# Eight stages of a four-layer block turned into two interleaved sequences of steps, with PSUM banks assigned by function

## The chip, the core and the metric

The kernel runs on one core of one Trainium2 chip. The metric is the device time of one execution in microseconds (us). The core's engines each work through their own instruction list in order and meet only at semaphores: TensorE (PE; its weight loads are shown as PEld), VectorE (DVE), ScalarE (ACT), GpSimd (POOL) and SyncE (SP), which here only issues DMAs. Matrix products land in PSUM, which has eight banks of 128 x 512 f32.

## The reference

The batch has 16 sequences of 128 tokens, 128 wide, with a context of the same shape. Four layers follow one another; each is a cross-attention and an FFN, each with a layer norm in front and a residual behind.

```
x = x + xattn0(ln(x), ctx)   # 8 heads of 64, softmax, output product
x = x + ffn0(ln(x))          # 8 experts of 64, top 2 by softmax, plus a shared one, silu
x = x + xattn1(ln(x), ctx)   # 16 heads of 8, softmax, no output product
x = x + ffn1(ln(x))          # 128-512-128, silu; inputs and weights quantized fp4 in blocks of 16
x = x + xattn2(ln(x), ctx)   # 16 heads of 8, masked softmax, output product
x = x + ffn2(ln(x))          # 128-128; fp8, ONE scale from the maximum over the whole tensor
x = x + xattn3(ln(x), ctx)   # 8 heads of 16, weights 1 + tanh(score), output product
x = x + ffn3(ln(x))          # rms norm, int8 rows, ternary weights, gelu, 128-512-128
```

Only the fp8 scale of ffn2 needs all sequences at once. Everything else is done sequence by sequence, so a sequence may be in layer 2 while another is in layer 0.

## The kernel before

The work is cut into one item for each sequence, 16 in all. There are **eight stages**, in the order of the reference, and a stage takes all 16 items before the next one starts, except that the first two items of a stage (EARLY) are mixed into the tail of the one before. Inside a stage `pipeline` (L212) unrolls the first four items, runs the middle in a hardware loop (Fori) of four steps a turn with addresses and semaphore values in registers, and unrolls the tail. In an attention stage the step k handles the projections of item k, the row maxima of item k-2, the probabilities of item k-3 and the output of item k-4.

Attention 1 and 2 compute every score twice. Once queries by keys (L414), from which DVE takes the row maxima (L1310, four of 128 x 512 for one item); and once keys by queries (L430), where the negative maximum is added by a second product with a selection matrix (L435), so that the exponential (L808, ACT) can be read straight from PSUM. The value products are L463. The f32 queries and keys are split into three bf16 parts (L854, L1325, L1021, L1023), written to DRAM by SP, and read back in stacked form. The keys and values of the context for all of layers 1 to 3 are projected in stage 0 (L587, L600) and prepared by DVE (L1399, L1420). Layer norms: DVE takes the statistics (L1279, L1281, L1283), POOL the inverse root (L994), DVE writes the normalized tile (L1288).

In ffn1 the block scales are computed on DVE (`block_scales`, L1143), the blocks are rounded in turn by POOL (L1059, L1049 to L1053) and DVE (`binades`, L1167, L1169 to L1173). In ffn2 DVE normalizes, takes maxima, POOL reduces them over the partitions (L1087), DVE quantizes (L1175).

PSUM: banks 0 and 1 take scores, 2 and 3 alternate for the transposed scores, 4 (and 5) values, 5 to 7 the rest; each stage deals them anew.

## Time and profile before

| what | value |
|---|---|
| median of 3 runs | 979.79 us (979.66 to 981.98) |
| profiled execution, first to last instruction (span) | 977.3 us |
| DVE busy | 629.9 us, 64% |
| PE busy | 614.2 us, 63% |
| ACT busy | 342.3 us, 35% |
| POOL busy | 329.3 us, 34% |
| DMA, mean share of 16 engines | 19.3% on the data queue |

The span is 2.5 us under the median of the runs. No engine is the bottleneck of the whole: the shares are averages over stages that are bound by different engines, so the profile is best read stage by stage. Roughly, from where each stage's own lines are busy, attention 0 runs to about 205 us, ffn0 to 318, attention 1 to 424, ffn1 to 592, attention 2 to 735, ffn2 to 779, attention 3 to 862, and ffn3 to 972.

### The profile page before, as it was taken

To read this page: it belongs to the slowest core of one execution; us is meant where nothing else is said; L and a number is where in the kernel's file an instruction comes from. 1 tells how busy PE (TensorE), PEld (TensorE's weight loads), DVE (VectorE), ACT (ScalarE), POOL (GpSimd) and SP (SyncE) were. 2 spreads that over 40 slices of the span, in tenths; PEclk is the share of its full clock that TensorE was granted. 3 is DMA by queue.
4 is the path that set the end of the run, shared out by engine and by line. 5 is a ranking of instruction groups with operands and counts; after the bars stand their busy time and mean duration, and the time that the engine had idled before them with its cause. 6 is when DMAs were issued, how large, how long until landed. Compare 5 with 4: busy or idle time off the path is not lost.

```text
span 977.3 us, 19947 instructions
## 1 busy us (share of the span) xinstructions
PE 614.2 (63%) x5798; PEld 435.2 (45%) x5804; DVE 629.9 (64%) x2044; ACT 342.3 (35%) x797; POOL 329.3 (34%) x560
## 2 busy tenths in 40 slices
PE   5699999878886899922122227999981276722331
PEld 3588888754444666601010015777750154511110
DVE  2576767637773788778888865666646523267774
ACT  2255555522221465521111112444430134422332
POOL 2112111145553222146656553222100123255441
PEclk9799999979996899965555556999995569955555
DMA  8422232200001344200000012322300135300001
GB/s 247 93 64 58 60 71 56 50 8 1 0 0 33 90 98 97 66 9 0 0 0 0 0 26 64 82 70 64 73 15 0 33 107 136 105 1 0 0 0 43
DMA packets 99780, 46.96 MB, mean 48 GB/s; under 512 B 82992, under 2 KB 92272, under 8 KB 99696
## 3 DMA queue, kind: packets, MB, share of 16 engines
q1 hardware_dynamic: 99728, 46.34, 19.3%
q8 instruction: 24, 0.39, 0.2%
q14 instruction: 28, 0.23, 0.1%
HBM read 26.39 MB, written 19.92 MB: 47 GB/s over the span
## 4 chain that ended last, share of the span: by engine, by line
PE 36%; issue 22%; DVE 13%; POOLq 11%; POOL 10%; DVEq 4%; ACT 2%; DMA 1%; SPq 0%; ACTq 0%
PE bank L463 3%; POOL stats L994 3%; PE bank L430 2%; PE bank L492 2%; PE bank L435 2%; PE bank L446 2%; PE bank L414 2%; POOLq L1050 2%; POOLq L1052 2%; POOL small L1072 2%; PE bank L424 2%; POOLq L1055 2%; POOL att_t L1059 2%; PE bank L565 2%; PE bank L487 1%
## 5 line engine op out<-in xcount | busy, mean ns | idle before, releaser
L994 POOL TENSOR_TENSOR stats<-stats,half_neg 128x1 f32<-128x1 f32 x112 | 63.3, 565 | 251.1 <-DVE stats L1283 243.8
L808 ACT ACTIVATE probs<-bank 128x512 f32<-128x512 f32 x160 | 95.2, 597 | 88.3 <-PE bank L435 87.6
L1310 DVE TENSOR_REDUCE mx<-bank 128x4 f32<-128x512 f32 x160 | 108.1, 680 | 9.7 <-PE bank L414 9.1
L430 PE MATMUL bank<-q_stack,k_stack 128*128 128x128 bf16 x512 | 72.6, 222 | 1.5 <-DVE shift_t L1344 1.4
L435 PE MATMUL bank<-shift_t,sel_bf 128*128 128x128 bf16 x512 | 72.2, 221 | 0.0
L657 PE MATMUL bank<-ident_bf,probs 128*128 128x128 bf16 x16 | 4.6, 286 | 105.5 <-POOL probs L1053 105.5
L1021 POOL CAST q_parts<-resid 128x128 bf16<-128x128 f32 x48 | 14.4, 300 | 149.5 <-DVE resid L1325 149.5
L1288 DVE TENSOR_SCALAR xn<-x_sb,stats 128x128 f32 (+1 forms) x96 | 37.3, 389 | 35.4 <-POOL stats L994 35.1
L1325 DVE SCALAR_TENSOR_TENSOR resid<-bank,w_bias_cols,q_parts 128x128 f32<-128x128 f32 x48 | 16.8, 350 | 64.6 <-ACT q_parts L854 63.9
L1294 DVE TENSOR_TENSOR x_sb<-bank,x_sb 128x128 f32 (+1 forms) x64 | 18.5, 289 | 61.9 <-PE bank L570 26.6
L430 PEld LDWEIGHTS bank<-q_stack,k_stack 128*128 128x128 bf16 x512 | 50.1, 99 | 7.4 <-issue 5.8
L463 PE MATMUL bank<-probs,v_slot 128*9 128x128 f32 x1024 | 52.4, 275 | 1.3 <-ACT probs L808 1.3
L414 PE MATMUL bank<-k_stack,q_stack 128*128 128x128 bf16 x512 | 50.4, 230 | 1.1 <-DMA q_stack<-scratch_q 0.8
L657 PEld LDWEIGHTS bank<-ident_bf,probs 128*128 128x128 bf16 x16 | 1.7, 104 | 110.9 <-POOL probs L1053 105.6
L435 PEld LDWEIGHTS bank<-shift_t,sel_bf 128*128 128x128 bf16 x512 | 50.8, 99 | 0.0
L487 PE MATMUL bank<-w_ident,xn 128*128 128x128 f32 x64 | 21.9, 342 | 45.2 <-DVE xn L1288 45.2
L751 PE MATMUL bank<-ident_bf,yq 128*128 128x128 bf16 x16 | 4.6, 286 | 69.7 <-DVE yq L1650 69.7
L904 ACT ACTIVATE yq_t<-bank 128x128 bf16<-128x128 bf16 x16 | 4.4, 277 | 120.8 <-PE bank L657 120.8
L414 PEld LDWEIGHTS bank<-k_stack,q_stack 128*128 128x128 bf16 x512 | 39.4, 104 | 14.6 <-issue 5.9
L840 ACT ACTIVATE xn_t<-bank 128x128 f32<-128x128 f32 x64 | 17.7, 277 | 80.2 <-PE bank L487 80.2
L1279 DVE BATCH_NORM_STATS2 stats<-x_sb 128x6 f32 (+1 forms) x112 | 32.6, 291 | 13.4 <-DMA x_sb<-in_x 5.8
L859 ACT ACTIVATE att<-bank 128x512 f32<-128x512 f32 (+1 forms) x48 | 25.2, 526 | 39.2 <-PE bank L463 39.2
(272 smaller groups left out, 1845.5 us busy)
## 6 DMA issues: line engine op xcount, KB each, us to landing
k_stack<-scratch_k SPq DMA_DIRECT2D x48, 192.0 KB, 3.4
q_stack<-scratch_q SPq DMA_DIRECT2D x48, 192.0 KB, 3.2
scratch_k<-k_parts SPq DMA_DIRECT2D x48, 96.0 KB, 1.8
scratch_q<-q_parts SPq DMA_DIRECT2D x48, 96.0 KB, 1.8
scratch_k<-k_parts SPq DMA_DIRECT2D x48, 64.0 KB, 1.6
scratch_q<-q_parts SPq DMA_DIRECT2D x48, 64.0 KB, 1.8
scratch_k<-k_parts SPq DMA_DIRECT2D x48, 32.0 KB, 1.5
scratch_q<-q_parts SPq DMA_DIRECT2D x48, 32.0 KB, 1.6
```

Of the source, the lines that this page charges most:

```text
L414: last = mm(dst[:, j * T:(j + 1) * T], q_stack[:, s, h, :], k_stack[:, s, h, :], start=layer == 1, stop=True, skip_group_check=True)
L424: mm(dst[:, j * T:(j + 1) * T], mask_bf[:, s, :], neg_ident[:, :], start=(j == 0), stop=False, skip_group_check=True)
L430: last = mm(o, k_stack[:, s, h, :], q_stack[:, s, h, :], start=layer == 1, stop=False, skip_group_check=True)
L435: last = mm(o, sel[:, h * T:(h + 1) * T], shift_t[:, s, :], start=False, stop=True, skip_group_check=True)
L463: last = mm(bank[4][32 * j:32 * j + w, cols], v, probs[:, (s * U + u) % 4, j * T:(j + 1) * T], start=layer < 3, stop=True, skip_group_chec ...
L487: tr(dst[:, 0:T], xn[:, sA, :], ident[:, :]).then_inc(ln["xnT_ps"], 1)
L808: activation(probs[:, (sP * U + u) % 4, :], bank[2 + u % 2][:, :], ACT.Tanh if layer == 3 else ACT.Exp, scale=float(d) ** -0.5).then_inc(s ...
L859: activation(att[:, sD, 0:U * T], bank[4][:, 0:U * T], ACT.Copy).then_inc(sm["ot"], 1)
L994: tt(stats[:, s, 9:10], stats[:, s, 8:9], half_neg[:, :], ALU.pow).then_inc(ln_rstd, 1)
L1279: nc.vector.bn_stats(stats[:, s, 0:6], x_sb[:, t, :])
L1288: return ts(dst, x_sb[:, t, :], stats[:, s, 6:7], stats[:, s, 9:10], ALU.subtract, ALU.mult)
L1310: reduce(mx[:, sM, u * UNIT:(u + 1) * UNIT], bank[u % 2][:, :].rearrange("p (h k) -> p h k", h=UNIT), AX.X, ALU.max).then_inc(sm["mx"], 1)
```

## The change

The stages and hardware loops are gone; all is unrolled, in **two sequences of steps** with ffn2 between them.

- **First sequence** (28 steps on PE, 29 on ACT, 35 on DVE). In each PE step one item is in attention 0, another in ffn0 three steps behind, another in attention 1 (5 and 6 behind), another in ffn1 (7 to 10 behind) and another in attention 2 (10 to 12 behind). Item b thus meets all five kinds of work within 13 steps. The order of the pieces within a step is written out, and is a different one for each engine.
- **ffn2** afterwards, all 16 items in four groups. Statistics and normalization of a group are done in the first sequence as soon as its items are through.
- **Second sequence** (26 steps on PE): attention 3 and, 7 to 10 steps behind, ffn3.
- **PSUM by function**: banks 0 and 1 scores, 2 transposed scores of every layer, 3 everything that comes in (context and query products, transposes of normalized tiles), 4 everything that goes out, 5 and 6 gate and up products, 7 the rest of the FFNs. `take` makes PE wait for the reader of a bank's last content before it writes there again.
- The shifts by the row maxima are no longer added by a product of their own: two more rows are put into the stacked queries by a DMA and ones into the stacked keys, so that one product with 50 rows gives the shifted score (L526 of the new kernel; L435 goes). The scores for the maxima are done in pairs in the two halves of the rows.
- Keys and values of layers 1 to 3 are projected in each layer's own step (`keys_values`) in place of stage 0, split together with the queries by ACT (`near_parts`, `far_parts`), DVE (`rest`) and POOL (`split`). The biases of values and outputs are added to x by POOL.
- The normalized tiles of the first sequence and of attention 3 are written by ACT (`normalized`) in place of DVE. The sums of attention 0 come from the exponentials' accumulators. The softmax of the router uses ACT's Exp in place of POOL's power.
- The fp4 rounding (`fp4_blocks`) is six DVE operations, POOL has no part in it.

```diff
-        def pipeline(eng, step, last, first=0, early=None, after=0):
...
-            for t in range(first, SLOTS):
-                step(t, t, 0)
-            with eng.Fori(0, B // SLOTS - 1) as i:
-                for j in range(SLOTS):
-                    step(i * SLOTS + (SLOTS + j), SLOTS + j, i + 1)
-            for t in range(B, B + last):
-                step(t, t, t // SLOTS)
-                if early and 0 <= t - B - after < EARLY:
-                    early(t - B - after, t - B - after, 0)
...
-                        last = mm(o, sel[:, h * T:(h + 1) * T], shift_t[:, s, :], start=False, stop=True,
-                                  skip_group_check=True)
...
-            pipeline(pe, attention_step(0), 4, early=ffn0_step(), after=2)
-            turn_weights()
-            pipeline(pe, ffn0_step(), 4, first=EARLY, early=attention_step(1))
-            pipeline(pe, attention_step(1), 4, first=EARLY, early=ffn1_step(), after=2)
-            pipeline(pe, ffn1_step(), 4, first=EARLY, early=attention_step(2))
-            pipeline(pe, attention_step(2), 4, first=EARLY)
-            ffn2(attention_step(3))
-            pipeline(pe, attention_step(3), 4, first=EARLY, early=ffn3_step(), after=2)
-            pipeline(pe, ffn3_step(), 4, first=EARLY)
...
-                        if k == 6:
-                            weights4_round(c - 1)
...
         bank = [ctx.enter_context(nc.psum_tensor(f"bank{i}", [P, 512], F32)) for i in range(8)]
         bank_bf = [b[:, :].bitcast(BF16) for b in bank]
+        SC, ST_BANK, IN_BANK, OUT_BANK = (bank[0], bank[1]), bank[2], bank[3], bank[4]
...
+            def take(name, reader, value):
+                if name in emptied:
+                    pe.wait_ge(*emptied[name])
+                emptied[name] = (reader, value)
...
+                take("in", A[l]["kv"], 2 * item(l, b) + 2)
+                mm(IN_BANK[:, 2 * T:3 * T], proj[:, 2 + l, :], ctx_all[:, b, :], start=True, stop=True)
+                mm(IN_BANK[:, 3 * T:4 * T], ctx_all[:, b, :], proj[:, 5 + l, :], start=True, stop=True
+                   ).then_inc(A[l]["kv_ps"], 1)
...
+                take("st", A[l]["p"], unit(l, b) + u + 1)
...
+                rows = slice(64 * (u % 2), 64 * (u % 2) + 50)
+                for j in range(UNIT):
+                    h = UNIT * (u // 2) + j
+                    done = mm(ST_BANK[:, j * T:(j + 1) * T], stack[l][rows, c, 1, h, :], stack[l][rows, c, 0, h, :],
+                              start=l == 1, stop=True, skip_group_check=True)
+                done.then_inc(A[l]["st"], 1)
...
+            for s in range(28):
+                scores(2, s - 12, 1)
+                values_out0(s - 2, 0)
+                turn(1, s - 5)
+                values_out0(s - 2, 1)
+                query(1, s - 5)
+                hidden_turn_f0(s - 4)
+                scores_t(1, s - 6, 0)
+                down_f1(s - 10)
+                shift_turn(2, s - 12)
+                keys0(s)
+                scores_t(1, s - 6, 1)
+                scores0(s - 1)
+                att_turn0(s - 2)
+                scores_t(1, s - 6, 2)
+                shared_turn_f0(s - 4)
+                values0(s)
+                project0(s - 2)
+                scores_t(1, s - 6, 3)
+                down_f0(s - 4)
+                if s == 6:
+                    for g in range(3):
+                        weights_turn(g)
+                scores_t(2, s - 12, 0)
+                values_out(1, s - 6, 0)
+                values_out(1, s - 6, 1)
+                turn0(s)
+                values_out(1, s - 6, 2)
+                values_out(1, s - 6, 3)
+                scores_t(2, s - 12, 1)
+                turn_f0(s - 3)
+                up_f1(s - 8)
+                scores_t(2, s - 12, 2)
+                route_f0(s - 3)
+                keys_values(2, s - 10)
+                out_turn(1, s - 6)
+                scores_t(2, s - 12, 3)
+                gate_f0(s - 3)
+                turn_f1(s - 7)
+                values_out(2, s - 12, 0)
+                values_out(2, s - 12, 1)
+                scores(1, s - 5, 0)
+                values_out(2, s - 12, 2)
+                values_out(2, s - 12, 3)
+                gate_f1(s - 7)
+                probs_turn0(s - 1, 0)
+                scores(1, s - 5, 1)
+                out_turn(2, s - 12)
+                query0(s)
+                scores(2, s - 11, 0)
+                hidden_turn_f1(s - 9)
+                att_turn2(s - 12)
+                up_f0(s - 3)
+                turn(2, s - 10)
+                shift_turn(1, s - 5)
+                project2(s - 12)
+                query(2, s - 10)
+                probs_turn0(s - 1, 1)
+                if s == 3:
+                    value_bias_product()
+                keys_values(1, s - 4)
+            for s in range(26):
+                turn_f3(s - 7)
+                values_out(3, s - 5, 0)
+                down_f3(s - 10)
+                values_out(3, s - 5, 1)
+                gate_f3(s - 7)
+                hidden_turn_f3(s - 9)
+                project3(s - 5)
+                turn(3, s - 1)
+                query(3, s - 1)
+                scores_t(3, s - 4, 0)
+                keys_values(3, s)
+                scores_t(3, s - 4, 1)
...
+                for j in range(UNIT):
+                    h = u * UNIT + j
+                    done = activation(probs_q[:, u, j * T:(j + 1) * T], SC[u][:, j * T:(j + 1) * T], ACT.Exp,
+                                      scale=float(D0) ** -0.5, bias=mx0[:, b % 2, H0 + h:H0 + h + 1],
+                                      accum_out=sums0[:, b % 2, 2 * j + u:2 * j + u + 1])
+                done.then_inc(A0["ex"], 1)
...
+                act.wait_ge(A[l]["rstd"], j + 1)
+                wait(act, A[l]["xT_ps"], j - 1)
+                activation(xn[l][:, j % 2, :], x_sb[:, b, :], ACT.Identity, bias=stats_a[l][:, j % 4, 10:11],
+                           scale=stats_a[l][:, j % 4, 9:10]).then_inc(A[l]["xn"], 1)
...
+                activation(parts[l][:, j % 2, 0, :, :], qk[l][:, j % 2, :, :], ACT.Copy).then_inc(A[l]["near"], 1)
...
+                activation(parts[l][:, j % 2, 1, :, :], resid[l][:, j % 2, :, :], ACT.Copy).then_inc(A[l]["far"], 1)
...
+            for s in range(29):
...
+                chances_f0(s - 4)
+                turned_f1(s - 8)
+                out_copied(2, s - 13)
+                gate_f0(s - 4)
+                gate_f1(s - 8)
+                normalized(2, s - 11)
+                probabilities0(s - 2, 0)
...
+                normalized_f0(s - 3)
+                probabilities(1, s - 6, 0)
+                far_parts(1, s - 5)
+                probabilities(1, s - 6, 1)
+                hidden_turned_f0(s - 4)
...
+                tt(cols[:, 8:9], cols[:, 7:8], ln_eps[:, :], ALU.add)
+                pool.drain()
+                tt(cols[:, 9:10], cols[:, 8:9], half_neg[:, :], ALU.pow)
+                pool.drain()
+                ts(cols[:, 10:11], cols[:, 6:7], cols[:, 9:10], -1.0, ALU.mult, ALU.mult).then_inc(done, 1)
...
+            def fp4_blocks(src, dst, work, magic, n, sc, rs):
+                tt(blocks(work, n), blocks(src, n), per_block(rs, n), ALU.mult)
+                drain()
+                ts(magic.bitcast(U16), work.bitcast(U16)[:, 1::2], EXPONENT >> 16, None, ALU.bitwise_and)
+                drain()
+                ts(magic, magic, 1.0, FP4_MAGIC, ALU.max, ALU.mult)
+                drain()
+                stt(work, work, -FP4_MAX, magic, ALU.max, ALU.add)
+                drain()
+                tt(work, work, magic, ALU.subtract)
+                drain()
+                return stt(blocks(dst, n), blocks(work, n), FP4_MAX, per_block(sc, n), ALU.min, ALU.mult)
...
+                tt(resid[l][:, j % 2, :, :], qk[l][:, j % 2, :, :], parts[l][:, j % 2, 0, :, :], ALU.subtract
+                   ).then_inc(A[l]["rest"], 1)
```

**ACT.** In the stages of before ACT runs one kind of function at a time. Attention 1 in its loop, one item (`probs` are the probabilities by Exp; `xn_t`, `q_parts` and `att` are copies):

```order
L859 ACTIVATE att<-bank4 128x512
L210 REGISTER_ALU
L804 REGISTER_ALU
L808 ACTIVATE probs<-bank2 128x512
L837 REGISTER_ALU
L840 ACTIVATE xn_t<-bank6 128x128
L210 REGISTER_ALU
L804 REGISTER_ALU
L808 ACTIVATE probs<-bank3 128x512
```

The changed kernel, in a step in which all five kinds of work are under way (`gate` and `gate4` are Silu of ffn0 and ffn1, `probs1` is Exp of attention 1; `oc2` belongs to attention 2, `small` to the router, by Exp):

```order
L1009 ACTIVATE small<-small 128x8
L1048 ACTIVATE yq_t<-bank7 128x128
L980 ACTIVATE oc2<-bank4 128x512
L1017 ACT_TABLE_LOAD
L1017 ACTIVATE gate<-from_x 128x64
L1019 ACTIVATE gate<-bank5 128x512
L1055 ACTIVATE gate4<-bank6,w_scale 128x512
L911 ACTIVATE xn2<-x_sb,stats2 128x128
```

and, 14 rows later in the same step,

```order
L953 ACTIVATE parts1<-qk1 128x256
L994 ACTIVATE xn_f<-x_sb,stats_f 128x128
L968 ACT_TABLE_LOAD
L968 ACTIVATE probs1<-bank2 128x512
L960 ACTIVATE parts1<-resid1 128x256
```

Silu now stands between exponentials, with a table load on each side: 42 table loads in the kernel's list where there were 6. Register instructions and branches are gone.

**DVE.** In before, one step of ffn1, between the scales of two blocks:

```order
L1165 TENSOR_TENSOR small<-small,gs4 128x40
L270 REGISTER_ALU
L1296 ISA
L1296 SCALAR_TENSOR_TENSOR x_sb<-bank7,w_scale,x_sb 128x128
L270 REGISTER_ALU
L1279 ISA
L1279 BN_STATS stats<-x_sb 128x6
L1281 BN_AGGR stats<-stats 128x2
L1283 TENSOR_SCALAR stats<-stats 128x1
L1169 TENSOR_SCALAR att_t<-att_t 128x640
L1171 TENSOR_SCALAR att_t<-att_t 128x640
L1173 TENSOR_SCALAR att_t<-att_t 128x640
```

In the changed kernel, the same place in a full step:

```order
L1379 TENSOR_TENSOR small4<-small4,gs4 128x40
L1655 TENSOR_TENSOR x_sb<-bank7,x_sb 128x128
L1385 TENSOR_TENSOR a4<-src4,small4 128x640
L1387 TENSOR_SCALAR b4<-a4 128x640
L1389 TENSOR_SCALAR b4<-b4 128x640
L1391 SCALAR_TENSOR_TENSOR a4<-a4,b4 128x640
L1393 TENSOR_TENSOR a4<-a4,b4 128x640
L1395 SCALAR_TENSOR_TENSOR dst4<-a4,small4 128x640
L1681 SCALAR_TENSOR_TENSOR src4<-bank5,w_scale,gate4 128x512
```

Six operations of 640 columns stand where three stood; the residual of ffn0 (L1655) lies between two pieces of ffn1.

**PE.** In before, attention 1: transposed scores and shifts in turn, into banks 2 and 3 alternately:

```order
L435 MATMUL bank2<-shift_t,sel_bf 128x128
L537 MATMUL bank5<-w_ident,att 128x128 x4
L476 REGISTER_ALU
L487 MATMUL bank6<-w_ident,xn 128x128
L210 REGISTER_ALU
L414 MATMUL bank0<-k_stack,q_stack 128x128 x4
L430 MATMUL bank3<-q_stack,k_stack 128x128
```

In the changed kernel, near the beginning of a full step (L421 are attention 0's value products, L462 and L470 attention 1's turn and query, L632 and L687 those of ffn0 and ffn1, L360 attention 0's keys):

```order
L462 MATMUL bank3<-w_ident,xn1 128x128
L421 MATMUL bank4<-early,probs0 128x64 x4
L470 MATMUL bank3<-xn_t1,w_proj 128x128
L632 MATMUL bank5<-w_ident,hid 128x128 x4
L526 MATMUL bank2<-stack1 128x128 x4
L687 MATMUL bank7<-wd1_q,hq_t 128x128 x4
L501 MATMUL bank0<-ident_bf,shift2 32x128
L360 MATMUL bank3<-ctx_all,w_wk0 128x128 x4
L526 MATMUL bank2<-stack1 128x128 x4
```

Pieces of five kinds of work follow one another. Consecutive transposed scores (L526) all go to bank 2; between two fills of it stand products of other items.

## Rows read from the trace of the kernel before

**Rows 1.** The windows view by stage: start and end, stretch, busy of each engine.

```profile
core 0: us, PE busy (x) PEld busy (x) DVE busy (x) ACT busy (x) POOL busy (x), PEclk, DMA share, GB/s
0.00:52.00 52.00, 30.99 (x166) 24.20 (x167) 21.11 (x70) 14.92 (x42) 10.93 (x26) 0.87 0.62 165
52.00:205.00 153.00, 142.08 (x1122) 121.57 (x1120) 104.80 (x322) 82.55 (x232) 32.43 (x41) 0.97 0.25 57
205.00:318.00 113.00, 87.52 (x391) 51.41 (x389) 69.95 (x344) 27.55 (x72) 53.62 (x55) 0.89 0.03 8
318.00:424.00 106.00, 90.53 (x1396) 66.07 (x1394) 83.98 (x257) 57.71 (x109) 23.34 (x61) 0.95 0.35 83
424.00:592.00 168.00, 39.01 (x183) 16.85 (x188) 132.19 (x319) 27.19 (x53) 103.47 (x94) 0.50 0.03 7
592.00:735.00 143.00, 133.42 (x1800) 98.32 (x1798) 83.83 (x252) 61.01 (x125) 27.35 (x72) 0.95 0.24 59
735.00:779.00 44.00, 6.80 (x39) 4.41 (x38) 27.84 (x77) 3.68 (x8) 6.33 (x12) 0.50 0.05 13
779.00:862.00 83.00, 53.97 (x555) 38.20 (x556) 26.08 (x107) 32.75 (x77) 25.57 (x69) 0.85 0.40 105
862.00:972.00 110.00, 29.87 (x157) 14.14 (x158) 79.74 (x299) 34.94 (x80) 46.27 (x132) 0.50 0.00 0
```

**Rows 2.** The page, part 4: the chain that ended last, by engine.

```profile
PE 36%; issue 22%; DVE 13%; POOLq 11%; POOL 10%; DVEq 4%; ACT 2%; DMA 1%; SPq 0%; ACTq 0%
```

**Rows 3.** The view by lines: operation, count, busy us and mean ns, idle before.

```profile
L1288 DVE TENSOR_SCALAR xn<-x_sb,stats 128x128 f32 (+1 forms) x96 | 37.3, 389 | 35.4 <-POOL stats L994 35.1
L1288 DVE TENSOR_SCALAR v<-x_sb,stats 128x128 f32 (+1 forms) x16 | 15.8, 987 | 0.7 <-POOL stats L994 0.7
L1283 DVE TENSOR_SCALAR stats<-stats 128x1 f32<-128x1 f32 x112 | 17.2, 154 | 9.2 <-issue 0.8
L1399 DVE TENSOR_TENSOR v<-bank,w_bias_rows 128x128 f32 (+1 forms) x48 | 11.0, 284 | 11.3 <-PE bank L587 11.1
L1385 DVE COPY gated<-bank 128x512 f32<-128x512 f32 x16 | 10.8, 678 | 0.7 <-PE bank L580 0.7
L1420 DVE SCALAR_TENSOR_TENSOR resid<-bank,w_bias_cols,k_parts 128x128 f32<-128x128 f32 x48 | 13.9, 346 | 19.1 <-ACT k_parts L888 19.0
...
L1171 DVE TENSOR_SCALAR att_t<-att_t 128x640 uint32<-128x640 uint32 (+2 forms) x18 | 8.2, 457 | 1.4
L1185 DVE TENSOR_TENSOR tmp_a<-tmp_a,tmp_b 128x512 f32<-128x512 f32 x4 | 2.8, 692 | 0.3
```

**Rows 4.** The view by lines, shapes apart, one line in two shapes.

```profile
L1153 DVE TENSOR_SCALAR small<-small 128x40 uint32<-128x40 uint32 x14 | 14.5, 1035 | 1.1
L1153 DVE TENSOR_SCALAR small<-small 128x32 uint32<-128x32 uint32 x5 | 0.9, 181 | 0.4
```

**Rows 5.** Timeline of ACT in attention 0; the view by lines for a table load.

```profile
112.92 1.14 ACT L821 ACTIVATE tmp_b<-bank,mx 128x128 f32<-128x128 f32 x4
...
L808 ACT ACT_TABLE_LOAD x2 | 2.6, 1283 | 0.0
```

**Rows 6.** Timeline of PE: two steps of attention 0 begin; then attention 1.

```profile
107.24 0.95 PE L391 MATMUL bank<-gated,hid 64*128 64x128 f32 x14
...
117.13 1.16 PE L391 MATMUL bank<-gated,hid 64*128 64x128 f32 x16
...
344.87 0.22 PE L430 MATMUL bank<-q_stack,k_stack 128*128 128x128 bf16 x1
344.92 0.22 PE L435 MATMUL bank<-shift_t,sel_bf 128*128 128x128 bf16 x1
```

**Rows 7.** Timeline of DVE at ffn2's maximum: start, length, idle before.

```profile
747.65 0.15 DVE L1590 TENSOR_SCALAR w_all<-w_scale 128x1 f32<-128x1 f32 x1 [3.67 <-POOL w_scale L1087]
...
748.46 0.49 DVE L1179 TENSOR_SCALAR tmp_a<-v,w_scale 128x512 f32<-128x512 f32 x1
749.02 0.43 DVE L1181 TENSOR_SCALAR tmp_b<-tmp_a 128x512 uint32<-128x512 uint32 x1
```

**Rows 8.** Timeline of SP's queue: the last input load is issued.

```profile
22.04 0.50 SPq L308 DMA_DIRECT2D q_stack<-in_c_sel  x1
```

2521 lines of the change are left out of this document (1315 added, 1206 removed).

## The prediction

> **What bounds the kernel now.** I read the busy line of the page first, then the chain, then the windows by stage. The shares of the whole say little: DVE 64%, PE 63%, and the chain that ended last passes from engine to engine, with 36% on PE, 22% issue and the rest on DVE and POOL [rows 2]. By stage it is clear [rows 1]. In attention 0 and attention 2 PE is busy 142.1 of 153 and 133.4 of 143 us, so 93%: PE binds. In ffn1 DVE is busy 132.2 of 168 us and PE 39 at a granted clock of 0.50 (1.2 GHz): DVE and POOL hand one block back and forth. In ffn0 and ffn3 no engine is over 78%: these are chains of waits. So what is idle in one stage is the bound of another, and work of different stages laid side by side could fill it. Per item the first five stages take, by their rates: attention 0 10.1 us (two successive steps begin at 107.24 and, with its first two products already past, 117.13, so 9.9 to 10.1) [rows 6], ffn0 113/16 = 7.1, attention 1 6.6, ffn1 10.5, attention 2 8.9. Together about 43 us.
>
> **What one item costs each engine afterwards.** DVE first, since it gets the fp4 rounding. Its busy time up to 735 us is 21.1 + 104.8 + 70.0 + 84.0 + 132.2 + 83.8 = 495.9 us [rows 1]. From it go:
> the normalized tiles, 64 at 389 ns and all of the 15.8 us of ffn1, 40.7 us; the additions of epsilon, 80 at 154 ns, 12.3; the value biases, the copy of the keys and the context's rests, 11.0 + 10.8 + 13.9 = 35.7 [rows 3]. The query rests grow from 128 to 256 columns and small copies go, about 0 in sum. The three binade operations go with 3 x 8.2 = 25 us, of which the weights keep 4. In their place stand six operations of 640 columns for each of 18 blocks. An operation with two tensor inputs takes 692 ns for 512 columns, so about 0.83 us for 640; the two with one input about 0.49 (457 ns is the mean of that row, short blocks included). So 4 x 0.83 + 2 x 0.49 = 4.3 us, and with the four short blocks 70 us [rows 3]. Net +49.
> One small operation on 40 columns took 1035 ns in ffn1, and on 32 columns with the weights 181 ns [rows 4]: it waits for POOL's wide rounding operations, which are gone. That gives back 14 x 0.85 = 12 us and some 6 more on its neighbour.
> Sum: 495.9 - 40.7 - 12.3 - 35.7 + 49 - 18 = 438 us. Between two dependent operations the engine is idle about 0.07 us (748.46 + 0.49 to 749.02) [rows 7]; I count 39 such places an item, 47 us, with 4 for the weights. What POOL still does (about 9 us an item: powers, bias additions, splits, the router's weighting) will hold up some of DVE's operations; I take 1.5 us an item, between 0 and the 3 us that some 25 touching operations would give if a third met a POOL operation halfway; 24 us. In all 513, of which 35 are for the weights: **29.7 us an item**: attention 0 3.3, ffn0 4.0, attention 1 5.6, ffn1 10.3, attention 2 6.5.
> PE: 31.0 + 142.1 + 87.5 + 90.5 + 39.0 + 133.4 = 523.5 us busy [rows 1]. The 512 shift products go, at one every 0.055 us [rows 6] 28 us; ffn1 runs at twice the clock, -19; the paired scores save 14, layer 3's projections 7, the bias products 12, the tails of single products that now overlap more than 20. That leaves some 420, **26 us an item** at 2.4 GHz.
> ACT: 14.9 + 82.6 + 27.6 + 57.7 + 27.2 + 61.0 = 271 us [rows 1]. Added: 80 normalized tiles at 0.25, keys and values 2 x 16 x 0.5, near and far parts 64 x 0.35, accumulator reads 128 x 0.1 (four exponentials take 1.14 us back to back [rows 5]), and two table loads of 1.28 us a step [rows 5], 39 in the first sequence, 50 us. About 390, **24 us an item**. The loads are the price of putting Silu between exponentials; they are paid only where ACT is the last.
> So DVE binds a full step, with PE 4 us behind it.
>
> **From items to time.** The pipeline has 28 PE steps. I price a phase by its longest engine. Until the first regular step nothing can be faster than the loads: the last is issued at 22.04 us [rows 8] and lands some us later, and ACT waits for all of them in its second step: 28 us. Attention 0 alone: 2.5 steps at 10 (PE 8.2, with hand-overs), 25. With ffn0: 2.1 steps at 14.5, 30. With attention 1 and the weights on DVE (12.9 + 35/2.9): 2.9 steps at 25, 72. With ffn1: 3 at 23.2, 70. All five: 5.5 at 29.7, 163. Then attention 0 ends, 2.5 at 26.4, 66; ffn0, 2.1 at 22.4, 47; attention 1, 2.9 at 16.8, 49; attention 2 alone 3 at 8, 24. The six phases bound by DVE are 467 us; the others 107.
> The engine that binds a stage is busy 93% of it today [rows 1], so I multiply the 467 by 1.08: 504. End of attention 2 at **611** instead of 735.
> ffn2: 44 us today [rows 1], of which 10 are two early items of attention 3 and 3 the earlier groups' statistics, now under way before. The 3.67 us in which DVE waits for POOL's reduction [rows 7] stay. **31**.
> Second sequence: before, 83/16 = 5.2 and 110/16 = 6.9 us an item, 12.1 together [rows 1]. DVE's busy time is (26.1 + 79.7)/16 = 6.6 us, with wider rests and gaps 7.5; POOL 4.5 plus splits, biases and the longer root, about 6; ACT 4.2 plus 2.2; PE 5.2 and more if the clock stays at 0.5. Four engines at 6 to 7.5 us: I take 8.5 for a full step, nearer to the DVE bound than to 12.1. Seven steps of attention 3 alone at 5, nine full, five at 8, five of ffn3 alone at 5.5, and 5 us of output: 35 + 77 + 40 + 28 + 5 = **184**, against 198 today. Little is gained, as filling and emptying take twelve of 26 steps.
> 611 + 31 + 184 = 826 us of span; the runs lie 2.5 above the profiled span of 977.3. **Forecast 828.**
>
> **A rule against the change.** One row shows an operation with a single tensor input waiting for POOL, 1035 against 181 ns [rows 4]. The Trainium skill, page "SBUF — State Buffer", section "Who interferes with whom", says more: a DVE instruction with two SBUF inputs also waits for a GpSimd instruction that reads SBUF, and the one issued first blocks the other for its whole length. The change puts four such operations into every block, where POOL had done half of them itself. By the rule the wait would be towards 3 us an item, and the sum some 20 us longer, 848; without any such wait it would be 24 shorter, 804.
>
> **The rivals.**
> 1. DVE runs without gaps: no 8%, no port waits. 443 + 107 + 31 + 165 + 5, with 2.5: **754**. For it: PE and ACT have 4 to 6 us of slack in a full step, and five independent items fill gaps. Against: 93% is the best of any stage now. 0.17.
> 2. The in-order queues wait for one another, as every function has one bank and each engine its own order. A full step becomes 36 us (factor 1.22): 570 + 107 + 31 + 190 + 7 = **905**. For it: PE, ACT and DVE are all over 80% loaded, and ffn1, where two engines alternate, runs at 79%. Against: each item has a whole step for each hand-over. 0.20.
> 3. The other side, slower. Bank 2 is filled ten times a full step, at some 1.3 us a fill, PE, reader and two hand-overs; bank 3 ten times at 1.5; banks 0 and 1 seven times in 15. Beside one another, 15 us, they are hidden. One behind another, because one engine's order ties the ends of one chain to the start of the next, they make 43 us, no less than the 43 that the separate stages take. The time is then 467 x 43/29.7 = 676, + 107 + 31 + 195 + 5: **1016**. It decides from a full step of 41 us on (467 x 1.37 = 640 meets 977). For it: only that single banks offer no second buffer, where banks 2 and 3 alternated. Against: the PE rows of neighbouring fills belong to different items. 0.09.
> 4. The change does what it says, but both bounds cancel (full step 40 to 41): no measurable change, 0.02.
>
> **How the numbers follow.** The forecast's case, full step 30 to 34, has 0.52 and reaches from 790 to 870. The range that holds 8 in 10 takes in rivals 1 and 2: 750 to 918; it leaves out the slow end and the fastest. Faster by over 0.3% (about what a measurement of this kernel can tell from no change): 0.52 + 0.17 + 0.20 = 0.89. Within 0.3%: 0.02. Slower: 0.09.
>
> **What would show it.** Right: the last residual of attention 2 at about 610 us; DVE over 85% busy from 160 to 500 us; PE's clock near 0.9 there, where ffn1 now has 0.50; 42 table loads on ACT, without DVE waiting for their probabilities; maxima waiting for scores under 2 us a step. Rival 2 or 3: DVE's largest wait is for PE's scores or transposes, and a full step spans over 35 us. Wrong in size: a six-operation block longer than 4.5 us, or a second sequence with steps near 12. A much longer table load than 1283 ns, or fetching of the unrolled code showing as issue time on PE, would be a cost that the sum lacks.

## The result: 3.2% faster, not 15%

| | before | after |
|---|---|---|
| median of the runs | 979.81 us (979.66 to 981.98) | 948.65 us (946.48 to 953.94) |
| profiled execution, span | 977.3 us | 951.9 us |
| mean granted TensorE clock | 0.784 | 0.732 |

The ratio is 0.9685, 95% interval 0.9653 to 0.9716. The forecast was 828 us. The sign is right; 121 us of the gain are missing, and the time lies outside the range of 750 to 918. (The profiled executions of e2, e6 and e18 below took 1.6% longer than the fastest run of the same kernel, so their steps are read as upper bounds.)

The head of the page after: busy times, then some of the 40 slices.

```profile
PE 649.2 (68%) x5258; PEld 453.7 (48%) x5294; DVE 551.9 (58%) x1675; ACT 482.0 (51%) x1265; POOL 247.0 (26%) x618
...
PE   1775476788887889988877666676641476677662
...
DVE  1152666576777787887777666662226324444655
...
PEclk9997768698898999997977777655555555555565
...
PE 38%; issue 19%; DVE 13%; SPq 8%; ACT 7%; DVEq 5%; DMA 4%; POOL 3%; POOLq 3%; ACTq 0%
```

Read the slice rows of TensorE and VectorE from the left: a slice is 23.8 us, and only slices 11 to 22 (238 to 524 us) show what the change is for, both engines at 7 to 9 tenths. Left and right of them lie the filling and the emptying, and from slice 27 on (619 us) the clock is at 0.5, 1.2 GHz, nearly throughout. In the chain, SP's queue and the DMAs are now 12%, against 1% in [rows 2].

Windows of the kernel after, cut where the kinds of step change: the full steps, the emptying, its last four steps, ffn2, the second sequence. Columns as in [rows 1].

```profile
283.00:464.00 181.00, 156.07 (x1545) 112.72 (x1557) 141.22 (x411) 131.00 (x364) 49.80 (x123) 0.93 0.20 54
464.00:630.00 166.00, 120.43 (x1133) 78.01 (x1143) 113.23 (x305) 86.33 (x183) 32.64 (x81) 0.73 0.20 52
630.00:709.00 79.00, 48.81 (x381) 28.54 (x380) 25.74 (x75) 19.02 (x42) 7.36 (x17) 0.50 0.12 31
712.00:743.00 31.00, 5.28 (x36) 3.94 (x36) 19.73 (x47) 2.39 (x4) 1.86 (x4) 0.50 0.00 0
743.00:952.00 209.00, 127.72 (x772) 87.70 (x780) 97.29 (x369) 90.61 (x241) 85.05 (x240) 0.52 0.25 66
```

In the full steps TensorE is busy 86% and VectorE 78%. Between 630 and 709 us, with attention 2 alone, TensorE is busy 62% at half clock and no other engine a third of the time: nothing is loaded there, and yet a step takes 20 us.

The steps can be measured one by one, since every item passes each line once. I take the start of the query product of attention 0 (L385) for steps 0 to 12 and that of the output product of attention 2 (L577) for steps 13 to 27, and set them against the prediction's phases, its six bound by VectorE with their factor of 1.08:

| steps | what runs | predicted, us | measured, us |
|---|---|---|---|
| 0 | loads | 28 | 28.2 |
| 1, 2 | attention 0 | 25 | 21.6 |
| 3, 4 | + ffn0 | 30 | 40.2 |
| 5 to 7 | + attention 1, weights | 78 | 100.4 |
| 8 to 10 | + ffn1 | 76 | 76.3 |
| 11 to 16 | all five | 176 | 184.7 |
| 17, 18 | - attention 0 | 71 | 57.7 |
| 19, 20 | - ffn0 | 51 | 58.0 |
| 21 to 23 | - attention 1 | 53 | 60.9 |
| 24 to 27 | attention 2 alone | 24 | 81.0 |
| | sum (before rounding) | 611 | 709 |

A full step is 30.8 us where 29.7 x 1.08 = 32 was forecast. Of the missing 98 us 57 lie in the last four steps, 33 in steps 3 to 7. ffn2 took its 31. The second sequence took 209 instead of 184, 25 us more. (With the 3 us before ffn2 that is 126 us of span; the profiled execution was the longest of the four, 5 us over their median.) One more thing lies in the last row: the prediction counted three such steps of 8 us, and there are four.

### The profile page after: what moved, and what is told of

It is laid out like the page before. It is cut to its first block, busy times and chain, and to the rows that moved or that the text cites. A ratio compares the mean times of both kernels' runs of the same rounds, so it can differ in the third digit from the quotient of the medians.

```text
span 951.9 us, 17711 instructions
## 1 busy us (share of the span) xinstructions
PE 649.2 (68%) x5258; PEld 453.7 (48%) x5294; DVE 551.9 (58%) x1675; ACT 482.0 (51%) x1265; POOL 247.0 (26%) x618
## 4 chain that ended last, share of the span: by engine, by line
PE 38%; issue 19%; DVE 13%; SPq 8%; ACT 7%; DVEq 5%; DMA 4%; POOL 3%; POOLq 3%; ACTq 0%
SPq L291 3%; DMA stack<-scratch 3%; PE bank L526 2%; SPq L279 2%; PE bank L421 2%; PE bank L490 2%; PE bank L546 2%; PE bank L543 2%; SPq L313 2%; ACT probs L968 2%; PE bank L470 2%; PE bank L399 2%; PE bank L385 2%; PE bank L485 1%; PE bank L617 1%
## 5 line engine op out<-in xcount | busy, mean ns | idle before, releaser
L1244 POOL TENSOR_TENSOR parts<-resid,parts 128x256 bf16<-128x256 f32 x48 | 32.2, 670 | 180.9 <-ACT parts L960 180.9
L526 PE MATMUL bank<-stack 50*128 50x128 bf16 x512 | 62.0, 256 | 23.3 <-ACT probs L968 21.7
L526 PEld LDWEIGHTS bank<-stack 50*128 50x128 bf16 x512 | 34.9, 108 | 45.5 <-ACT probs L968 26.6
L521 PE MATMUL bank<-neg_ident,mask_bf 128*128 128x128 bf16 x256 | 32.8, 269 | 33.5 <-DMA stack<-shift_t 17.3
L551 PE MATMUL bank<-probs,v 128*9 128x128 f32 x1024 | 46.1, 318 | 1.8 <-DVE att L1595 1.7
L886 ACT ACTIVATE probs_q<-bank,mx 128x128 f32<-128x128 f32 x128 | 45.4, 380 | 0.0
L980 ACT ACTIVATE oc<-bank 128x512 f32<-128x512 f32 (+1 forms) x48 | 25.3, 527 | 36.0 <-PE bank L551 26.4
L490 PE MATMUL bank<-stack 48*128 48x128 bf16 x512 | 29.6, 244 | 17.9 <-DVE mx L1565 9.6
L521 PEld LDWEIGHTS bank<-neg_ident,mask_bf 128*128 128x128 bf16 x256 | 21.1, 118 | 42.6 <-ACT probs L968 19.1
L490 PEld LDWEIGHTS bank<-stack 48*128 48x128 bf16 x512 | 17.1, 104 | 46.4 <-issue 22.9
L1479 DVE BATCH_NORM_STATS2 stats<-x_sb 128x6 f32<-128x128 f32 x80 | 22.9, 287 | 23.8 <-ACT xn L911 23.6
L470 PE MATMUL bank<-xn_t,w_proj 128*128 128x128 f32 x96 | 27.6, 379 | 9.4 <-ACT xn_t L936 9.2
L551 PEld LDWEIGHTS bank<-probs,v 128*9 128x9 f32 x1024 | 26.1, 102 | 14.7 <-ACT probs L968 4.5
```

Of the source, the lines that this page charges most:

```text
L470: mm(IN_BANK[:, T:2 * T], proj[:, l - 1, :], xn_t[l][:, j % 2, :], start=True, stop=True).then_inc(A[l]["q_ps"], 1)
L490: done = mm(SC[u][:, j * T:(j + 1) * T], stack[l][rows, c, 0, 4 * pair + j, :], stack[l][rows, c, 1, 4 * pair + j, :], start=l == 1, stop= ...
L521: mm(ST_BANK[:, j * T:(j + 1) * T], mask_bf[:, b % 4, :], neg_ident[:, :], start=j == 0, stop=False, skip_group_check=True)
L526: done = mm(ST_BANK[:, j * T:(j + 1) * T], stack[l][rows, c, 1, h, :], stack[l][rows, c, 0, h, :], start=l == 1, stop=True, skip_group_che ...
L551: done = mm(OUT_BANK[32 * j:32 * j + D1 + 1, value_cols(u)], v[l][:, b % NA, first_head(u) + j, :], probs[l][:, n % 4, j * T:(j + 1) * T], ...
L886: done = activation(probs_q[:, u, j * T:(j + 1) * T], SC[u][:, j * T:(j + 1) * T], ACT.Exp, scale=float(D0) ** -0.5, bias=mx0[:, b % 2, H0 ...
```

## What a step with one item in it waits for

Timeline of TensorE in one of the last steps of the kernel after: start, length, line, in brackets the idle time before and what ended it.

```profile
632.62 0.29 PE L501 MATMUL bank<-ident_bf,shift 128*32 128x128 bf16 x1 [1.36 <-DVE shift L1576]
635.81 0.61 PE L521 MATMUL bank<-neg_ident,mask_bf 128*128 128x128 bf16 x4 [2.91 <-DMA stack<-shift_t]
636.35 0.60 PE L526 MATMUL bank<-stack 50*128 50x128 bf16 x4
637.64 0.61 PE L521 MATMUL bank<-neg_ident,mask_bf 128*128 128x128 bf16 x4 [0.69 <-ACT probs L968]
638.18 0.60 PE L526 MATMUL bank<-stack 50*128 50x128 bf16 x4
639.48 0.61 PE L521 MATMUL bank<-neg_ident,mask_bf 128*128 128x128 bf16 x4 [0.69 <-ACT probs L968]
```

The item is taken round once in a step: scores, maxima (1.36 us of waiting), their transposition, a DMA of 4 KB into the stack (2.91), four banks of transposed scores, each 1.8 us with TensorE and ScalarE taking turns on bank 2, then values, division and projection. Only when the projection is past do the next item's second scores follow in TensorE's order. Such a path, from a piece of one step to the same piece of the next, is called a **ring** here: its length divided by the steps it may take is a floor under the step, whatever the engines' load. The theory was that this ring (A) makes the 20 us. The rivals: TensorE's clock of 0.5 there (C), ScalarE's function tables (T), and VectorE's load in all steps (D), as the prediction had it.

All times below are medians with the ratio to the kernel before, run beside them on the same chip; the changed kernel's own ratio is 0.9685. A step of the drain is the mean of steps 24 to 27 unless said otherwise.

**e1, no function tables.**

```diff
-                activation(gate[:, b % 2, 0:512], G_BANK[:, :], ACT.Silu)
+                activation(gate[:, b % 2, 0:512], G_BANK[:, :], ACT.Identity)
```

> Edit: the three Silu activations of ffn0 and ffn1 become Identity, so the function table is never switched in the first sequence; the FFN values are therefore not those of the reference, their shapes and places stay. The changed kernel took 948.65 us. Theory A (chains: a step with few items in it lasts as long as the chain of dependent pieces written into it, about 20 us for attention 2, whatever the engines' load): only the loads that lie on such a chain count, -10 to -20 us, so 928 to 939; the drain steps 24 to 27 stay at 20 us, for they have no table load. Rival T (the 39 table switches of ScalarE are what the sum had too cheap): 39 x 1.28 = 50 us or more come off, so at most 900. Rival D (VectorE's load sets every step): under 5 us, 944 to 949.

927.41 us, ratio 0.9452 (0.9414 to 0.9490). Some 23 us came off, 15 of them in steps 11 to 16 (184.7 to 169.6) and 8 in steps 8 to 10; the drain stayed at 20.0. Rival T falls as the main cause, but the loads were not free either, as the prediction had assumed. The view by lines of the kernel after, for the three lines that load most, and ScalarE's timeline around one load:

```profile
L968 ACT ACT_TABLE_LOAD x18 | 23.1, 1283 | 0.3
L1017 ACT ACT_TABLE_LOAD x16 | 20.5, 1283 | 0.3
L1055 ACT ACT_TABLE_LOAD x4 | 5.1, 1283 | 0.1
...
290.95 0.28 ACT L1048 ACTIVATE yq_t<-bank 128x128 bf16<-128x128 bf16 x1 [0.23 <-PE bank L653]
291.25 1.28 ACT L1017 ACT_TABLE_LOAD   x1
292.54 0.26 ACT L1017 ACTIVATE gate<-from_x 128x64 f32<-128x64 f32 x1
```

These are 38 loads and 48.7 us of ScalarE; less than half shows in the time. But it is not spread evenly. Two loads a step, 18 in steps 8 to 16, are 23.1 us, and these nine steps lost 23.4: there ScalarE's loads came off whole, with ScalarE busy 72%. The 23 other loads of the first sequence gave some 3 us. (The Trainium skill, page "ScalarE: Activation LUTs", section "What ACT_TABLE_LOAD costs", adds a drain of about 1380 ns to each, so 2.66 us for a switch; for the 42 loads of this trace that would be an estimated 112 us of ScalarE. The trace does not agree: the operation behind the load starts 1.31 us after the one before it has ended, 291.23 to 292.54, and the steps lost 1.3 us a load.)

**e2, no wait for the shifts; e3, idle products to hold the clock; e4, the next item's scores earlier.**

```diff
-                if not live(b):
+                if b not in range(NA):
                     return
                 sp.wait_ge(A[l]["shT"], b + 1)
...
                 shift_turn(2, s - 12)
+                idle(8, s, SC[1])
...
                 up_f1(s - 8)
+                if s >= SW:
+                    scores(2, s - 11, 0)
```

(One hunk of each. e3 has such idle products at six places of a step, 18 in all where the expectation says 16, e4 moves the second scores and the shift's transposition as well.)

> Edit: the rows of the maxima are loaded into the stacks for the first four items of layers 1 and 2 only and stay there; the score products of later items wait for no shift DMA (the maxima, their transposition and copy are still computed). The values of the softmax are the same up to rounding as long as nothing overflows. Theory A (chains): in the drain the path from scores over maxima, shift, transposition and DMA to the transposed scores is cut, about 6 us of 20.5 a step; steps 20 to 27 go to 14 to 16 us each, -35 to -45 us in all, 905 to 915. Rival C (the drain is slow because TensorE is granted 1.2 GHz there): the path is cut but TensorE's work stays, a step stays above 18 us: 930 or more. Rival D (load of VectorE): no difference, 945 to 950.

> Edit: from PE step 22 on products that nobody reads (128 x 128 f32, into bank 1) stand where TensorE waits for the shift DMA and for the probabilities, 16 a step, and 82 more stand before and in ffn2 (bank 7). Rival C (clock): the granted clock is 1.0 instead of 0.5 from step 23 on; the products on the chain of a drain step take 13 of its 20.3 us at 1.2 GHz, so steps 23 to 27 fall to 14 us, -30 us, and if the clock then holds, the second sequence falls from 208 us by another 20: 900 to 920. Theory A (chains) in its strict form, where hand-overs and not products make the 20 us: no step gets shorter than 18 us, 940 to 955. If the clock stays at 0.5 the run says nothing on either.

> Edit: from PE step 22 on both score products and the shift transposition of the next item of attention 2 stand among the current item's transposed scores and values instead of after its projection, and VectorE takes its maxima before the current item's division and residual; the same work in another order. Theory A (chains): scores, maxima, shift and DMA of one item now lie beside the transposed scores of the other, -5 us in each of six steps, -30 us, 915 to 922. Rivals C (clock) and D (load): the same work at the same clock, 943 to 950.

e2: 938.35 us, ratio 0.9510 (0.9437 to 0.9583); the drain step went from 20.25 to 17.9 us, not to 14 to 16. e3: 943.60 us, ratio 0.9588 (0.9545 to 0.9631); the granted clock rose to 0.83 (621 to 690 us) and the step fell to 18.0, while ffn2 got 10 us longer with its idle products, and the second sequence ran at 0.50 again, 177.5 against 176.7 us from its first residual to its last. Each is a part of the 20 us and none the whole. e4 went the other way: **969.44 us**, ratio 0.9861 (0.9820 to 0.9901), with three steps of 24.9 us and a last one of 12.7, in which no next item stands beside the item. TensorE in such a step of e4, and the transfers that it waits for on SP's queue:

```profile
641.08 0.39 PE L471 MATMUL bank<-xn_t,w_proj 128*128 128x128 f32 x2
...
654.28 1.04 PE L486 MATMUL bank<-mask_bf,neg_ident 128*128 128x512 bf16 x2 [9.42 <-DMA stack<-scratch]
...
644.35 2.96 SPq L292 DMA_DIRECT2D scratch<-parts  x6
648.44 3.08 SPq L314 DMA_DIRECT2D stack<-scratch  x4
```

Here is a second ring, which the theory had not seen. From the query product (641.08) over ScalarE's, VectorE's and GpSimd's splitting, six DMAs out to DRAM and four back, each issue about 0.5 to 0.8 us of SP, to the scores (654.28) it takes 13.2 us. In the changed kernel's order it has a whole step for that and is nearly hidden. The edit moved the scores up by half a step, and the DMA ring, left with less, stretched the step to 25. Theory A was right in kind, and the edit drawn from it wrong, because it shortened one ring by taking room from another.

**e13, e14, e17, e18: the two rings cut one at a time.** Items 12 to 15 of layer 2 use the stacks of items 8 to 11, without save and load (e13); with e2's edit beside it (e14); with e4's order (e17); e14 with idle products (e18).

```diff
             def save(l, b):
-                if not live(b):
+                if not live(b) or l == 2 and b >= LAST:
                     return
```

> Edit: items 12 to 15 of layer 2 are neither saved to nor loaded from DRAM; their scores use the stacks of items 8 to 11 and wait for no load. Two-ring theory (a step of the drain is the longer of two rings: over shift and projection 20.3 us, over query, DMA out and in 18.2 us): the longer one stays, steps 24 to 27 remain at 19.5 to 20.5 us. If instead the round trip through DRAM set the step, they fall to 16 or less.

> Edit: as the run without the round trip, and the shift rows of the first four items stay as in e2. Two-ring theory: with each cut alone the other ring holds the step at 20 and at 18; with both cut steps 24 to 27 fall to 13 to 15 us, what TensorE's own work takes there at 1.2 GHz (38.8 us in the 60 up to 700, so 13 a step) with the waits for ScalarE. If e2's 18.2 was set by anything else (ScalarE's hand-overs, the clock), they stay at 17 to 18.5.

> Edit: the order of e4 and, as in e13, no save and no load for items 12 to 15 of layer 2. If e4's steps of 25 us are the ring query, DMA out, DMA in, scores, which that order left half a step shorter to run in, they fall with the round trip gone, to 14 to 16 us, below the 20.3 of the changed kernel's own order, since scores and shift of one item now lie beside the other's transposed scores. If the order itself made the engines wait (a bank or an in-order queue), they stay above 20.

> Edit: both rings cut as in e14, and the idle products of the drain (14 a step, in bank 1, from step 21). TensorE's work in a step of e14 is some 12 us at 1.2 GHz on a path of 17.3. If the clock sets what is left and rises to 0.9 or more, that halves: 17.3 to 12 us a step. If the hand-overs do, and the idle products take back what the clock gives (14 x 0.2 us), 15 to 17 us.

The residual of attention 2, one row for each run: after, e2, e4, e13, e14, e17. From the first to the last start are four steps.

```profile
L1609 DVE TENSOR_TENSOR x_sb<-bank,x_sb x5: 291/292/292, 628.9 to 709.9; 128x128 f32<-128x128 f32 x5
L1609 DVE TENSOR_TENSOR x_sb<-bank,x_sb x5: 291/292/292, 624.9 to 696.6; 128x128 f32<-128x128 f32 x5
L1619 DVE TENSOR_TENSOR x_sb<-bank,x_sb x5: 291/292/292, 641.3 to 728.5; 128x128 f32<-128x128 f32 x5
L1610 DVE TENSOR_TENSOR x_sb<-bank,x_sb x5: 291/292/292, 621.0 to 700.2; 128x128 f32<-128x128 f32 x5
L1610 DVE TENSOR_TENSOR x_sb<-bank,x_sb x5: 291/292/292, 613.9 to 683.1; 128x128 f32<-128x128 f32 x5
L1620 DVE TENSOR_TENSOR x_sb<-bank,x_sb x5: 291/291/292, 628.3 to 695.8; 128x128 f32<-128x128 f32 x5
```

| drain step, us | DMA ring there | DMA ring cut |
|---|---|---|
| order of the change | 20.25 | 19.8 (e13) |
| no shift wait | 17.9 (e2) | 17.3 (e14) |
| scores earlier | 24.9 (e4, first three of the four) | 16.3 and 16.0 (e17, steps 25 and 26) |

With the DMA ring cut, e4's order has the shortest steps of the three, 16 us once it runs. That settles what held e4 up. It is no recommendation: from the output product of step 20 to that of step 27 the change takes 142 us, e13 140, e17 136 and e14 128, for in e17 the step in which the order changes (22) takes 27.5 us instead of 19.1. The times, two runs each: e13 945.37 us, ratio 0.9629 (0.9577 to 0.9682); e14 931.79, 0.9491 (0.9426 to 0.9557); e17 942.25, 0.9612 (0.9538 to 0.9686).

e13 and e17 cannot be told from the change itself by their intervals; the argument here rests on the steps.

But e14's expectation fell: with both cut the step stays at 17.3, not 13 to 15. e18, two runs of 927.37 and 942.50 us (the profile is of the second), raises the clock to 0.89, and its step takes 16.9. Its timeline shows where the clock's gain went: with no wait left behind the shift's transposition, the eight idle products (two records each) stand in the path themselves.

```profile
649.94 0.29 PE L502 MATMUL bank<-ident_bf,shift 128*32 128x128 bf16 x1 [1.28 <-DVE shift L1587]
650.16 3.56 PE L757 MATMUL bank<-w_ident 128*128 128x128 f32 x16
653.55 0.39 PE L522 MATMUL bank<-neg_ident,mask_bf 128*128 128x128 bf16 x4
```

What the 20 us are made of can be read from windows over the four steps: after, e14, e18, and of e18 the idle products alone; below them TensorE's waits in the kernel after, 628 to 709 us.

```profile
628.00:709.00 81.00, 50.68 (x386) 29.65 (x386) 26.27 (x77) 19.85 (x44) 7.36 (x17) 0.50 0.11 30
613.00:682.00 69.00, 50.39 (x386) 29.61 (x386) 26.05 (x77) 19.74 (x44) 7.38 (x17) 0.50 0.00 1
629.00:697.00 68.00, 57.15 (x533) 42.62 (x531) 27.01 (x78) 20.00 (x45) 7.36 (x17) 0.90 0.00 1
629.00:697.00 68.00, 28.35 (x144) 23.91 (x144) 0.90 0.00 1
...
PE bank L521 <- DMA stack<-shift_t: 11.5, 4, 2.9
PE bank L521 <- ACT probs L968: 6.9, 10, 0.7
PE bank L501 <- DVE shift L1576: 6.5, 4, 1.9
PE bank L562 <- ACT oc L980: 3.2, 4, 0.8
```

TensorE's own work is 12.7 us of the step (50.68 in four) and its waits are 7.5: 2.9 for the shift's DMA, 1.7 for the probabilities, 1.6 for the maxima, 1.3 for copies and the division. In e14 the work is the same, 12.6, and only the 2.9 are gone: 12.6 and the other 4.7 are its 17.3. In e18, at a clock of 0.90, the work without the idle products is 57.15 less 28.35, so 7.2 us a step (records of neighbouring products overlap, so it may be a little more). The clock thus costs about 5 us of a drain step and the waits 7.5: rival C and theory A both hold in part, and the clock costs more than any single wait. A step of e14 with this clock and without the idle products would take 12 to 13 us; that is an estimate from these rows, and no run shows it.

## The first steps and the one-off work

**e5, without the reductions by GpSimd; e10, the one-off work earlier.**

```diff
-                nc.gpsimd.partition_all_reduce(w_all[:, 0:4], w_stats[:, 0:4], P, bass.bass_isa.ReduceOp.max)
...
+                nc.gpsimd.tensor_copy(w_all[:, 0:6], w_stats[:, 0:6]).then_inc(prep["all"], 1)
...
-                if s == 5:
+                if s == 2:
                     weight_stats()
```

> Edit: the two reductions over the partitions by GpSimd in its step 5 become a copy (the weight scales are then not those of the reference), and the ones in the key stack of layer 2, two GpSimd memsets of 32 x 4096, are written by VectorE after the last weight. Theory A (a step is as long as the longest path in it): steps 4 and 9 (28.6 us for the step that ends at the fourth query) lose the 13 us in which GpSimd holds the reciprocal roots back, and the step with 36.0 us loses the 2 x 3.5 us in which VectorE's small operations wait for the memsets: 36.0 to 29 and 28.6 to 16, -20 us, 928 to 933 on the scale of the changed kernel's 948.65. Rival D (VectorE's weight work sets these steps): only the 7 us of the memsets go, 940 to 943.

> Edit: ScalarE waits for the last loads in its step 5, not 1; the statistics and roots of items 0 to 3 stand at the start; the weight maxima come in VectorE's step 2 and the reductions in GpSimd's step 2; the weight scales and blocks follow in VectorE's steps 4 to 7, one each; the ones of layer 2's key stack are written by VectorE. Theory A (one-off work and late loads lie on the longest path of steps 0 to 7): the first query product starts at about 20 us instead of 28, the reductions no longer hold up a root (28.6 to 16 us in one step, as measured without them), and the blocks lie in steps with room: -35 us, 905 to 920. Rival D (the work is the same, so the steps are as long, only others): -8 for the loads and no more than -10 beside it, 930 to 940.

GpSimd in step 4 of the kernel after. The library's reductions show as short rows; the idle time around them is what they take.

```profile
63.81 1.04 POOL L1261 TENSOR_TENSOR gate<-gate,small 128x512 f32<-128x512 f32 x1 [5.73 <-ACT gate L1019]
70.44 0.39 POOL L1267 PARTITION_ALL_REDUCE w_all<-w_stats  x1 [5.58 <-issue]
70.75 0.48 POOL L1268 PARTITION_ALL_REDUCE w_all<-w_stats  x1
78.31 0.18 POOL L1187 TENSOR_TENSOR stats_f<-stats_f,ln_eps 128x1 f32<-128x1 f32 x1 [7.08 <-issue]
```

From 64.86 to 78.31, 13.5 us, nobody gets a root from GpSimd, and ScalarE waits 14.1 us for one. e5 took 938.09 us, ratio 0.9558 (0.9510 to 0.9606): step 4 fell from 28.6 to 15.9 us, as expected. The memsets, 7 us on paper, gave 0.3 us in their step (36.0 to 35.7) and 1.2 in steps 5 to 7. VectorE takes as long for them: in e10

```profile
118.05 3.47 DVE L1858 MEMSET stack<- 32x4096 bf16 x1 [0.96 <-DVE w_q L1473]
```

e10 took 930.21 us, ratio 0.9510 (0.9480 to 0.9541), -17 us where -35 was expected. The first query product starts at 16.8 instead of 28.2 us, but steps 1 and 2 give most of that back, 29.2 against 21.6. The wait there, from 17 to 36 us:

```profile
DVE w_stats L1413 <- DMA stack<-in_w32T: 17.0, 1, 17.0
```

With the weight maxima in its step 2 VectorE itself stands waiting for the last load, and the first maxima of attention 0 behind it: the wait was moved from ScalarE to VectorE. Steps 3 and 4 stayed (40.5), for step 3 grew to 18.4 as step 4 fell; steps 5 to 7 gained 12.

## The full steps, and the second sequence

**e6, five fp4 operations fewer; e7, no mask products; e15, both with e1.**

```diff
-                fp4_blocks(src4[:, k % 4, cols], dst4[:, k % 2, cols], a4[:, cols], b4[:, cols], n, tiles[1], tiles[3]
-                           ).then_inc(F1S["hh"], 1)
+                tt(blocks(dst4[:, k % 2, cols], n), blocks(src4[:, k % 4, cols], n), per_block(tiles[3], n), ALU.mult
+                   ).then_inc(F1S["hh"], 1)
...
-                    for j in range(UNIT):
-                        mm(ST_BANK[:, j * T:(j + 1) * T], mask_bf[:, b % 4, :], neg_ident[:, :],
-                           start=j == 0, stop=False, skip_group_check=True)
```

> Edit: of the six operations of the fp4 rounding in a regular block only the first stays (it writes the rounded tile directly, unrounded; the FFN values of ffn1 are not those of the reference). VectorE loses five operations, 3.0 us an item. Rival D (VectorE binds the full step, as the prediction said): the full steps 11 to 16 fall from 30.8 to 27.8 us and the others with ffn1 too, -3 us in 16 steps, -45 us. Theory A with TensorE as the bound of the full step (busy 45 of 50 us there, VectorE 40): at most 1 us a step, -15 us or less; 934 to 948 on the scale of 948.65.

> Edit: the products that add the mask to the scores of attention 2 are left out (4 of 128 x 512 and 16 of 128 x 128 an item; its softmax is then unmasked). TensorE loses some 2.6 us an item at 2.4 GHz, 4.4 us at 1.2 GHz. If TensorE binds the full step: steps 13 to 16 fall by 2 to 2.6 us each, and in the drain, where these products lie on the chain, steps 24 to 27 by 3 to 4 us: -30 to -40 us in all, 909 to 919. Rival D (VectorE binds the full step): the full steps stay, only the drain gains, -20 us, 929 or more.

> Edit: no Silu tables (as e1), one fp4 operation of six (as e6), no mask products (as e7), all at once. Alone they took 15, 6 and 6 us off the six full steps 11 to 16 (184.7 us). If the full step is shared between the engines in turn, the sum appears or a little more, 150 to 158 us; if another path of hand-overs lies right below, it stops at 165 or more.

| | time, us | ratio | steps 11 to 16, us |
|---|---|---|---|
| after | 948.65 | 0.9685 | 184.7 |
| e1, ScalarE relieved | 927.41 | 0.9452 (0.9414 to 0.9490) | 169.6 |
| e6, VectorE relieved | 940.66 | 0.9583 (0.9541 to 0.9625) | 178.4 |
| e7, TensorE relieved | 928.14 | 0.9453 (0.9398 to 0.9507) | 178.3 |
| e15, all three | 901.15 | 0.9179 (0.9130 to 0.9228) | 168.5 |

3.0 us less of VectorE in an item and 2.6 us less of TensorE each took 1 us off a full step; neither engine alone binds it. The 2.6 us less of ScalarE in e1 took 2.5 off: of the three it is ScalarE, busy 72%, whose work lay on the path. All three together give hardly more than e1 alone: 28 us a step. What holds it there is not settled: TensorE is still busy 90% in e15 (280 to 380 us), but so it was with the mask products, so that busy time is no proof of a bound. e7's larger gain is in the drain: 17.1 us a step.

**e11, silu by tanh.** Identity in e1 only measured; this form keeps the values.

```diff
-                activation(gate[:, b % 2, 0:512], G_BANK[:, :], ACT.Silu).then_inc(F0S["sl"], 1)
+                activation(gate[:, b % 2, 0:512], G_BANK[:, :], ACT.Tanh, scale=0.5).then_inc(F0S["sl"], 1)
...
+                stt(g[:, 0:512], g[:, 0:512], 1.0, G_BANK[:, :], ALU.add, ALU.mult).then_inc(F0S["gd"], 1)
```

> Edit: silu(x) is computed as x/2 (1 + tanh(x/2)): ScalarE takes the tanh, which needs no other function table than the exponential here (2 table loads in the program, 42 before), VectorE one more operation of 512 columns in each of ffn0 and ffn1 and one of 64. Theory T (the 25 us that went with the switches are to be had without leaving anything out): -25 from the loads, +1.6 us an item on VectorE, of which a third shows, as for the relief of VectorE that gave a fifth: -15 to -22 us, 927 to 934. Rival D (VectorE binds the full step): +1.6 us in 16 steps takes back all of it, 945 to 955.

947.35 us, ratio 0.9688 (0.9654 to 0.9723): nothing gained. In its profiled execution steps 8 to 16 are 6 us shorter, where e1 had 23, and steps 5 to 7 are 3 us longer. Steps 11 to 16 take 179.8 us, against 169.6 in e1: 1.7 us a step came back. The new operations stand between ScalarE and the readers of its result, in ffn0 GpSimd; that they cost so much more than a relief of VectorE (e6) gave, because they lengthen this path, is argued from the order and not shown.

**e8 and e9, two guesses at the ring of the second sequence.**

```diff
                 values_out(3, s - 5, 1)
+                project3(s - 5)
...
-                    wait(act, A[3]["vb"], b - 1)
-                    activation(v_raw[:, b % 2, :], IN_BANK[:, 3 * T:4 * T], ACT.Copy).then_inc(A[l]["kv"], 1)
+                    wait(act, A[3]["vb"], b - 3)
+                    activation(v_raw[:, b % 4, :], IN_BANK[:, 3 * T:4 * T], ACT.Copy).then_inc(A[l]["kv"], 1)
```

> Edit: in the second sequence the output product of attention 3 stands right behind its value products, ahead of ffn3's gate product and hidden transposition. Theory A: the step of 10.6 us there is a ring, residual, norm and quantization on VectorE, transposition, copy by ScalarE, gate product, output product, residual; with the output product ahead of the gate the ring loses the transposition, its copy and the gate product: 10.6 to about 9.3 us in 13 steps, -15 us, 930 to 937. Rival C (TensorE at 1.2 GHz, busy 7.8 of 10.6 us, sets it): no change beyond 3 us, 945 to 949.

> Edit: the raw values of layer 3 have four buffers instead of two, so ScalarE's copy waits for GpSimd's bias addition of three items before, not one before. Theory B (the second sequence's step of 10.6 us is a ring through that buffer: value products on TensorE, bias addition on GpSimd, ScalarE's copy, ScalarE's copy of the transposed tile behind it, gate product, output product, residual): ScalarE's wait for GpSimd, 17 us in 70, goes and the step falls to 9.5, -13 us, 933 to 939 on the scale of the changed kernel's 948.65. Rival C (TensorE at 1.2 GHz is the bound there): under 4 us, 945 to 949.

e8: 952.64 us, ratio 0.9732 (0.9697 to 0.9766), no gain, if anything half a per cent slower; its ring was not the one. e9: 934.92 us, ratio 0.9521 (0.9460 to 0.9582), 16 us faster by the ratio. The waits of the kernel after from 780 to 850 us, and the windows of the same stretch, after and e9:

```profile
ACT probs L924 <- POOL probs L1235: 21.4, 6, 4.4
...
780.00:850.00 70.00, 46.54 (x273) 32.22 (x277) 32.07 (x122) 31.70 (x86) 30.28 (x87) 0.50 0.26 70
...
780.00:850.00 70.00, 47.95 (x331) 32.03 (x334) 38.41 (x148) 38.86 (x105) 35.31 (x99) 0.67 0.31 83
```

ScalarE's copy of the raw values waited 3.6 us a time for GpSimd to have emptied one of two buffers, and everything behind it on ScalarE with it. With four buffers steps went from 10.6 to 12.6 us down to 8.4 to 10.3, and the part from the first residual to the last from 176.7 to 159.2 us. The clock rose to 0.67 with no edit aimed at it, so a part of these 17.5 us may have come through the clock; no run separates the two.

**e12 and e16, what helped put together.**

> Edit: the three edits of this group together, and the idle products of the drain (from step 21, none in ffn2). If the terms are independent: -13 -35 -18 -10, 870 to 885. If the early work, the tables and the ring were hiding one another, less than 50 us in all, 900 or more.

> Edit: four buffers for the raw values (e9), the early work (e10), the idle products of the drain from step 21 on, and from item 12 on every other transposed score of attention 2 in bank 5, free by then; Silu as in the changed kernel. Without the tanh form, which gained nothing (e11), the first three come to what e12 gave, 900 us. The second bank takes three waits of 0.69 us off a step if the ring over the shift still sets it, -6 us: 892 to 898; nothing if the round trip does, at 18: 898 to 903.

e12, the edits of e9, e10 and e11 with the idle products of the drain, takes **901.70 us**, ratio 0.9213 (0.9186 to 0.9240): 8% under the kernel before and 4.9% under the change. It is the fastest version that leaves nothing out. By the ratios that is 46 us under the change; e9 (16), e10 (17), e11 (0) and the idle products of e3 (10) give 43 singly, so the terms roughly add up, and the expected 870 to 885 missed because the single ones did. e16, without the tanh and with a second bank for the transposed scores of the last four items, takes 909.18 us, ratio 0.9230 (0.9171 to 0.9289), the same. Its drain step is 18.8 us, 18.0 in e12. The second bank gave nothing, but this is no test of the single bank: in e12 the idle products already stand where TensorE waited for the probabilities (none of that wait is left there), and in e16 TensorE waits 5.2 us in the four steps for the stacks' loads instead.

## Why the prediction was right or wrong

- **Work of an item.** VectorE's busy time in the first sequence was forecast at 438 us and is 434.8 (the windows to 712 us), ScalarE's at 390 and is 389.0. TensorE's 420 became 516: the forecast took it at 2.4 GHz throughout. Weighted by the granted clock of each window (22.8 x 0.97, 64.1 x 0.80, 103.2 x 0.86, 156.1 x 0.93, 120.4 x 0.73, 48.8 x 0.50) the 516 are an estimated 420, so the clock can account for all of the difference, with some 57 us of it from 464 us on. Within the terms, the six operations of a block of 640 columns take 4.1 us and not 4.3, and ScalarE's normalized tiles 0.48 us and not 0.25.
- **Port waits.** The 24 us are not there, about 7 are. A wide operation with two tensor inputs has the same length at its median as at its maximum:

```profile
L1391 DVE SCALAR_TENSOR_TENSOR a<-a,b x18: 293/825/826, 185.1 to 638.5; 128x640 f32<-128x640 f32 x14, 128x128 f32<-128x128 f32 x2, 128x512 f32<-128x512 f32 x2
L1630 DVE CAST small<-top x16: 170/172/3540, 61.5 to 507.2; 128x8 f32<-128x8 uint32 x16
```

  The second row is the exception: one cast of eight elements took 3.54 us beside a GpSimd memset of 3.50, and the operation behind it (L1632, 128x8) 3.55 beside the next memset. So the 848 us of the rule in the Trainium skill ("SBUF — State Buffer", "Who interferes with whom") did not come. That does not speak against the rule: of the 14 blocks of 640 columns only one met a GpSimd operation, L1244 with two inputs at 547.2 us, and there L1385 took 1.07 us where 0.81 is usual and L1244 0.73 where 0.67 is. The order kept them apart, which the forecast had not asked. The row that waited most is a cast, which the same section counts among the operations that can take the shared pair of ports.
- **Which engine binds.** "So DVE binds a full step" failed. The step's length was right (30.8 against 32), but relieving VectorE by 3 us gave 1. VectorE is busy 78% (75% from 160 to 500 us, where over 85% was to show it right).
- **The step that failed most** is "I price a phase by its longest engine". In a full step load and hand-overs come to nearly the same, so the error did not show there. In a step of attention 2 alone the load was priced at 8 us and the step takes 20.25: 7.5 us are waits that nothing else fills, since one item's pieces follow one another, and some 5 are the same work at 1.2 GHz. The text had the ring's pieces (rival 3 counts the fills of bank 2) but asked of them only whether they add up in a full step.
- **The drain** was the mis-sized term, 24 against 81 us. Of the 57 us 30 are waits (7.5 a step), 19 are TensorE's work at 1.2 GHz (12.7 where 8 was taken), and 8 are the fourth step that the sum did not count. The ring over the shift and the projection is the longest there, the one over DRAM a little shorter.
- **Attention 1 and weights, with ffn0 before**: 108 predicted, 140.6 measured. 13 us are GpSimd's reductions (e5), whose rows read 0.4 us; the rest, some 20, is put down to weight blocks in the path of the items, of which e10's gain of 12 us in steps 5 to 7 shows a part.
- **Table loads** "paid only where ACT is the last": they cost 23 us (e1), nearly all of it in steps 8 to 16, though ScalarE is busy 72% in full steps. The count, 42, was right.
- **Second sequence**: full steps of 8.5 predicted, 10.6 to 12.6 measured, 17 of the 25 us by a pair of buffers (e9), with what the clock's rise gave among them. The sum by engines had no term for engines that take turns on one buffer. The prediction named steps near 12 as the sign of this error.
- **Rivals.** No rival had the time: it lies 44 us over rival 2's 905 and 31 under no change. Rival 2's mechanism did not come where it was placed, for full steps stayed under 36 us; waits of queues for one another there are, but in the steps that are not full. Rival 1, an engine without gaps, did not come. Rival 3 did not come: no full step reached 41 us, and TensorE's weight loads waited for the reader of bank 2 only 8.7 us in the 181 of the full steps. Faster at all had 0.89, and that came true for less than its reasons: of the gain forecast in the first sequence (735 to 611) a fifth came.

## What to carry to other kernels

A wavefront's full step came out right here when priced by its busiest engine, by luck as much as by reason, since relieving that engine gave a third of the relief; its first and last steps must be priced by the longest path from a piece of one step to the same piece of the next, DMAs, issue times and the clock that the waits leave TensorE included; with 16 items and a lag of 12, such steps were 524 of the first sequence's 709 us. Before pieces are moved to shorten one such ring, measure the second longest: an edit that gives one ring room takes it from another, and cutting each alone and both together shows which holds. And when a buffer of two is shared by three engines, look at the wait rows of the engine that is not busy: two more buffers were worth 1.6% here.

## What had not been expected of the hardware

- A GpSimd reduction over the partitions shows as 0.4 us and keeps GpSimd from other work for 6 to 7 us: two of them, 13.5 us, of which e5 gave back 12.7.
- A memset of 32 x 4096 in bf16 takes 3.47 us on VectorE and 3.50 on GpSimd; moving two of them gave 1 us (e5).
- A function table load holds ScalarE for 1.31 us in all, 1.28 of it the load itself, and the next operation follows 0.01 us later.
- Idle products (18 a step, eight of them in 3.56 us) held the granted clock at 0.83 to 0.90 (2.4 GHz for most of the stretch) where it was 0.50. TensorE's own work in a drain step fell from 12.7 to about 7 or 8 us by it, but the products took 7 themselves, so the step of 20 gained only 2; after ffn2, whose stretch had 0.77 with them, it was 0.50 again in the second sequence, and it rose to 0.67 there in e9 with shorter waits and no such products.
- On SP six saves take 2.96 us and four loads 3.08 to issue; with their landings they are most of the 13.2 us of the round trip through DRAM.
